# Slot records five chunks behind, more DMAs at the seams of the tail, and three tiles of types and masks in the message phase

## What is computed

```python
edge_index = jnp.stack([src, dst])
x = _layernorm(x + _L0_gnn_ref(x, edge_index, edge_attr_8, ...), axis=-1)     # attention, 8 heads
x = _layernorm(x + _L1_gnn_ref(x, edge_index, edge_type_16, ...), axis=-1)    # messages with an edge type of 16
x = _layernorm(x + _L2_gnn_ref(x, node_vec1, src, dst, edge_attr_4, edge_attr_8, ...), axis=-1)
x = _layernorm(x + _L3_gnn_ref(x, edge_index, L3_gnn_hyperedge_weight, ...), axis=-1)
```

```python
x = x @ W.T
e = segment_sum(Binv[edge_idx][:, None] * x[node_idx], edge_idx, num_segments=N_EDGES)
out = segment_sum(Dinv[node_idx][:, None] * e[edge_idx], node_idx, num_segments=N_NODES)
```

## Time and profile before

| | us |
|---|---|
| median of 3 runs (2760.82 to 2774.23) | 2763.07 |
| the profiled execution's own time | 2763.75 |
| its span, first to last instruction | 2762.0 |
| busy: PE / DVE / ACT / POOL | 1485.9 / 1676.3 / 879.7 / 1997.8 |

### The profile page before, as it was taken

One profiled execution on the slowest core, in us unless ns is written; L12 is line 12 of the kernel. 1 busy time (PEld: TensorE's weight loads), 2 busy tenths in 40 slices (PEclk: granted clock), 3 DMA queues, 4 the chain that ended last, 5 costly groups with the idle time before them and its releaser, 6 DMA issues. The chain is left out here.

```text
span 2762.0 us, 22483 instructions
## 1 busy us (share of the span) xinstructions
PE 1485.9 (54%) x4577; PEld 756.9 (27%) x4577; DVE 1676.3 (61%) x5026; ACT 879.7 (32%) x1963; POOL 1997.8 (72%) x1591
## 2 busy tenths in 40 slices
PE   6676548888736555554687736756663122221121
PEld 1233224444412222221333313422221121221110
DVE  8999837788916666684877754534444244334443
ACT  0111116666724455553466531211111111110000
POOL 5777677777358877764877727868887688878787
PEclk9989869999967677776889868978886555555555
DMA  1111133444244454444556547867887454443331
GB/s 25 16 27 28 21 93 110 124 126 114 69 110 120 101 119 121 114 90 102 100 133 145 129 104 211 263 193 224 230 226 182 104 124 122 116 109 83 85 85 45
DMA packets 357529, 320.56 MB, mean 116 GB/s; under 512 B 107129, under 2 KB 311824, under 8 KB 357377
## 3 DMA queue, kind: packets, MB, share of 16 engines
q1 hardware_dynamic: 256593, 247.94, 32.6%
q0 software_dynamic: 100800, 71.18, 13.8%
HBM read 222.19 MB, written 96.95 MB: 116 GB/s over the span
## 5 line engine op out<-in xcount | busy, mean ns | idle before, releaser
L2019 PE MATMUL tl_pX<-k_ident,tl_ga 125*128 125x125 f32 x400 | 92.4, 375 | 447.4 <-DMA tl_ga<-table_TE,k_s_idxE 256.3
L438 POOL DMA_INDIRECT tl_ga<-table_TE,k_s_idxE x200 | 245.5, 1228 | 80.3 <-issue 56.4
L2130 DVE TENSOR_TENSOR_SCAN tl_S<-tl_same,tl_S,tl_pX 128x500 f32<-128x500 f32 x96 | 120.2, 1252 | 244.8 <-issue 215.2
L2019 PEld LDWEIGHTS tl_pX<-k_ident,tl_ga 125*128 125x128 f32 x400 | 63.0, 192 | 465.4 <-DMA tl_ga<-table_TE,k_s_idxE 267.1
L438 POOL DMA_INDIRECT ms_ga<-table_T,k_idxS x100 | 140.5, 1405 | 65.1 <-issue 58.2
L1234 DVE TENSOR_TENSOR dr_o<-dr_x,tl_pMul 128x512 f32<-128x512 f32 x98 | 67.1, 685 | 185.8 <-DMA dr_x<-x 107.8
L1331 POOL DMA_INDIRECT k_pay<-table_ptab,k_clip x100 | 148.6, 1486 | 27.4 <-issue 27.1
L438 POOL DMA_INDIRECT at_ga<-x,at_srcI x100 | 130.3, 1303 | 43.2 <-issue 23.9
L438 POOL DMA_INDIRECT eq_ga<-table_T,k_idxS x100 | 125.6, 1256 | 48.7 <-issue 27.9
L438 POOL DMA_INDIRECT tl_ga<-table_TH,k_send x100 | 124.4, 1244 | 44.9 <-issue 44.2
L438 POOL DMA_INDIRECT at_gb<-x,at_dstI x100 | 126.5, 1265 | 38.8 <-issue 27.1
(11 more groups left out here) (430 smaller groups left out, 4726.4 us busy)
## 6 DMA issues: line engine op xcount, KB each, us to landing
dr_x<-x SPq DMA_DIRECT2D x97, 256.0 KB, 8.0
result<-dr_o SPq DMA_DIRECT2D x97, 256.0 KB, 5.4
dm_xT<-xT SPq DMA_DIRECT2D x32, 768.0 KB, 6.7
table_T<-at_y SPq DMA_DIRECT2D x50, 250.0 KB
table_T<-ms_y SPq DMA_DIRECT2D x50, 250.0 KB
table_T<-eq_y SPq DMA_DIRECT2D x50, 250.0 KB
tl_same<-table_dsame SPq DMA_DIRECT2D x50, 250.0 KB, 4.7
table_TE<-tl_y SPq DMA_DIRECT2D x50, 250.0 KB
```

Of the source, the lines that this page charges most:

```text
L438: nc.gpsimd.indirect_dma_start(out=buf[:, k, :], out_offset=None, in_=table, in_offset=bass.IndirectOffsetOnAxis(ap=index[:, CT * c + k:CT ...
L2019: last = nc.tensor.transpose(pX[j % 2][:, k * TP:(k + 1) * TP], ga[j % RG][:, k, :], K["ident"][0:TP, 0:TP])
L2130: nc.vector.tensor_tensor_scan(S[i][:], same[j % RM][:], pX[i][:, 0:CE], 0.0 if j % NC == 0 else S[1 - i][:, CE - 1:CE], ALU.mult, ALU.add ...
```

## The change

Three things. The message phase gets three copies of the types and of both masks instead of two, and SP issues them a turn earlier. The equivariant phase issues the slot records of a chunk five turns later (`LATE`), those of the last five chunks after the loop. In the tail four chunks of states instead of two stand at the first seam (`SEAM`), four chunks of scatters instead of two at the second, three instead of two at the third; the ring of o gets six copies, and the normalization of the target rows starts two turns earlier.

```diff
-        RG, RX, RU = 5, 4, 4
+        RG, RX, RU, RM = 5, 4, 4, 3
...
             def load_mask(c):
-                need(sp, s_S, c - 1)
-                need(sp, s_mean, c - 1)
-                sp.dma_start(same[c % 2][:], ...).then_inc(s_same[c % 2], 16)
-                sp.dma_start(deg[c % 2][:], ...).then_inc(s_same[c % 2], 16)
+                need(sp, s_S, c - RM + 1)
+                need(sp, s_mean, c - RM + 1)
+                sp.dma_start(same[c % RM][:], ...).then_inc(s_same[c % RM], 16)
+                sp.dma_start(deg[c % RM][:], ...).then_inc(s_same[c % RM], 16)
 
             def load_types(c):
-                need(sp, s_oneh, c - 1)
-                sp.dma_start(typ[c % 2][:], ...).then_inc(s_typ[c % 2], 16)
+                need(sp, s_oneh, c - RM + 1)
+                sp.dma_start(typ[c % RM][:], ...).then_inc(s_typ[c % RM], 16)
...
-            for s in range(-3, NC + 3):
-                if live(s + 3):
-                    load_types(s + 3)
-                if live(s + 1):
-                    load_mask(s + 1)
+            for s in range(-4, NC + 3):
+                if live(s + 4):
+                    load_types(s + 4)
+                if live(s + 2):
+                    load_mask(s + 2)
...
-        RG, RZ = 7, 4
+        RG, RZ, LATE = 7, 4, 5
...
-                if live(s):
-                    payload(s)
+                if live(s - LATE):
+                    payload(s - LATE)
+            for c in range(NC - LATE, NC):
+                payload(c)
             pool.wait_ge(s_pay, 16 * NT)
...
-        RG, RM, RL = 4, 3, 3
+        RG, RM, RL, RO = 4, 3, 3, 6
-        LN_EDGE = J_EDGE - 4
+        LN_EDGE = J_EDGE - 6
+        SEAM = 4
...
-            keep_states(0)
-            keep_states(1)
+            for c in range(SEAM):
+                keep_states(c)
             stored(pool, J_NODE)
             pool.wait_ge(s_zr, 16 * 2)
             for c in range(NC):
                 fetch(J_NODE + c)
-                if c + 2 < NC:
-                    keep_states(c + 2)
+                if c + SEAM < NC:
+                    keep_states(c + SEAM)
             for p in range(XR):
                 pool.wait_ge(dn.s_st[p], 16 * ((DQ - p + XR - 1) // XR + (p == (DQ - 1) % XR)))
-            scatter(0)
-            scatter(1)
+            for e in range(SEAM):
+                scatter(e)
             stored(pool, J_EDGE)
             for c in range(NC):
                 fetch(J_EDGE + c)
-                if c + 2 < NC - 2:
-                    scatter(c + 2)
-            scatter(NC - 2)
-            scatter(NC - 1)
+                if c + SEAM < NC - 3:
+                    scatter(c + SEAM)
+            for e in range(NC - 3, NC):
+                scatter(e)
             stored(pool, J_LAST)
```

More of the change, by code:

```diff
@@ L1252, in message_phase @@
         m, oF = (a.sb(n, [D, CE]) for n in ("m", "oF"))
-        xs, S, mean, same, deg = ([a.sb(f"{n}{i}", [D, CE]) for i in range(2)] for n in ("xs", "S", "mean", "same", "deg"))
-        typ, oneh = [a.sb(f"typ{i}", [16, CE], I32) for i in range(2)], [a.sb(f"oneh{i}", [128, CE]) for i in range(2)]
+        xs, S, mean = ([a.sb(f"{n}{i}", [D, CE]) for i in range(2)] for n in ("xs", "S", "mean"))
+        same, deg = ([a.sb(f"{n}{i}", [D, CE]) for i in range(RM)] for n in ("same", "deg"))
+        typ, oneh = [a.sb(f"typ{i}", [16, CE], I32) for i in range(RM)], [a.sb(f"oneh{i}", [128, CE]) for i in range(2)]
         n1, hg = (a.sb(n, [TP, 2 * CT, D]) for n in ("n1", "hg"))
@@ L1267, in message_phase @@
         s_ga, s_xt = [a.sem(f"ga{i}") for i in range(RG)], [a.sem(f"xt{i}") for i in range(RX)]
-        s_same, s_typ, s_st = ([a.sem(f"{n}{i}") for i in range(2)] for n in ("same", "type", "stored"))
+        s_same, s_typ = ([a.sem(f"{n}{i}") for i in range(RM)] for n in ("same", "type"))
+        s_st = [a.sem(f"stored{i}") for i in range(2)]
         block = ctx.enter_context(nc.Block())
@@ L1281, in load_mask @@
             def load_mask(c):
-                need(sp, s_S, c - 1)
-                need(sp, s_mean, c - 1)
-                sp.dma_start(same[c % 2][:], T["dsame"][:, CE * c:CE * c + CE].broadcast_to([D, CE])).then_inc(s_same[c % 2], 16)
-                sp.dma_start(deg[c % 2][:], T["rdeg"][:, CE * c:CE * c + CE].broadcast_to([D, CE])).then_inc(s_same[c % 2], 16)
+                need(sp, s_S, c - RM + 1)
+                need(sp, s_mean, c - RM + 1)
+                sp.dma_start(same[c % RM][:], T["dsame"][:, CE * c:CE * c + CE].broadcast_to([D, CE])).then_inc(s_same[c % RM], 16)
+                sp.dma_start(deg[c % RM][:], T["rdeg"][:, CE * c:CE * c + CE].broadcast_to([D, CE])).then_inc(s_same[c % RM], 16)
             def load_types(c):
-                need(sp, s_oneh, c - 1)
-                sp.dma_start(typ[c % 2][:], g["type_row"][:, CE * c:CE * c + CE].broadcast_to([16, CE])).then_inc(s_typ[c % 2], 16)
+                need(sp, s_oneh, c - RM + 1)
+                sp.dma_start(typ[c % RM][:], g["type_row"][:, CE * c:CE * c + CE].broadcast_to([16, CE])).then_inc(s_typ[c % RM], 16)
             def load_targets(c):
@@ L1463, in one_hot @@
             def one_hot(c):
-                dve.wait_ge(s_typ[c % 2], 16 * (c // 2 + 1))
+                dve.wait_ge(s_typ[c % RM], 16 * (c // RM + 1))
                 need(dve, s_psM, c - 1)
-                nc.vector.tensor_scalar(oneh[c % 2][0:16, :], typ[c % 2][:], kindf[:, 0:1], None, ALU.is_equal).then_inc(s_oneh, 1)
+                nc.vector.tensor_scalar(oneh[c % 2][0:16, :], typ[c % RM][:], kindf[:, 0:1], None, ALU.is_equal).then_inc(s_oneh, 1)
             def running(c):
@@ L1471, in running @@
                 dve.wait_ge(s_m, c + 1)
-                dve.wait_ge(s_same[i], 32 * (c // 2 + 1))
-                nc.vector.tensor_tensor_scan(S[i][:], same[i][:], m[:], 0.0 if c == 0 else S[1 - i][:, CE - 1:CE], ALU.mult, ALU.add).then_inc(s_S, 1)
+                dve.wait_ge(s_same[c % RM], 32 * (c // RM + 1))
+                nc.vector.tensor_tensor_scan(S[i][:], same[c % RM][:], m[:], 0.0 if c == 0 else S[1 - i][:, CE - 1:CE], ALU.mult, ALU.add).then_inc(s_S, 1)
             def averaged(c):
@@ L1478, in averaged @@
                 need(dve, s_psO, c - 1)
-                nc.vector.tensor_tensor(mean[i][:], S[i][:], deg[i][:], ALU.mult).then_inc(s_mean, 1)
+                nc.vector.tensor_tensor(mean[i][:], S[i][:], deg[c % RM][:], ALU.mult).then_inc(s_mean, 1)
             def residual(c):
@@ L1847, in tail_phase @@
         y = [a.sb(f"y{i}", [TP, CT, D]) for i in range(2)]
-        x, z, o = ([a.sb(f"{n}{i}", [TP, CT, D]) for i in range(RL)] for n in ("x", "z", "o"))
+        x, z = ([a.sb(f"{n}{i}", [TP, CT, D]) for i in range(RL)] for n in ("x", "z"))
+        o = [a.sb(f"o{i}", [TP, CT, D]) for i in range(RO)]
         st = a.sb("st", [TP, CT, 6])
@@ L1862, in tail_phase @@
         s_ga, s_same, s_fac, s_x, s_out, s_st = (
-            [a.sem(f"{n}{i}") for i in range(k)] for n, k in (("ga", RG), ("same", RM), ("fac", RM), ("x", RL), ("out", RL), ("stored", 2)))
+            [a.sem(f"{n}{i}") for i in range(k)] for n, k in (("ga", RG), ("same", RM), ("fac", RM), ("x", RL), ("out", RO), ("stored", 2)))
         s_gb, s_s4, s_rowT, s_row, s_rowst, s_rown, s_rowi, s_colT, s_idx, s_end, s_dinv, s_sl = (
@@ L1965, in scatter @@
             def scatter(e):
-                c, i = e % NC, e % RL
+                c, i = e % NC, e % RO
                 index = K["dst_end"] if e < NC else K["src_end"]
@@ L1973, in scattered @@
             def scattered(n):
-                for i in range(RL):
-                    pool.wait_ge(s_out[i], 64 * ((n - i + RL - 1) // RL))
+                for i in range(RO):
+                    pool.wait_ge(s_out[i], 64 * ((n - i + RO - 1) // RO))
             for c in range(NC):
@@ L2168, in finish @@
                 dve.wait_ge(s_mv, e + 1)
-                need(dve, s_out[e % RL], 64 * (e // RL))
-                normalize(nc, o[e % RL], z[e % RL], CT, mv[i], rs[i]).then_inc(s_o, 1)
+                need(dve, s_out[e % RO], 64 * (e // RO))
+                normalize(nc, o[e % RO], z[e % RL], CT, mv[i], rs[i]).then_inc(s_o, 1)
             def batch_norm():
```

## The result

The changed kernel took 2724.54 us (median of 4 runs, 2719.83 to 2730.55) beside 2765.7 for the kernel before on the same chip: a ratio of 0.9849, 95% interval 0.9814 to 0.9885, so 41 us less where 53 were forecast, and inside the range of the likeliest case (2692 to 2732). The profiled executions stand 44.0 us apart (spans 2762.0 and 2718.0).

A forecast was written before the change was run, and what follows sets the result against it. The prediction took a one-turn loop between types and y to bound the message phase, and POOL the edge stage. Terms -38 + 0 + 2 - 17 = -53 gave 2710 us; range 2692 to 2732, with neighbouring cases 2688 to 2742.

The forecast's parts named there:

- likeliest case: Whole kernel: message phase -24 to -53 and seam 3 -12 to -18, so 2692 to 2732 us; chance 0.50.
- Part 1: Message phase, three tiles of types and masks: types loop spans two turns, POOL becomes the bound by little; -38 us.
- best case: Message phase: POOL loses its 28.5 us of waits and DVE's lag behind the last gather shrinks; 53 us gained.
- worst case: Message phase: more POOL rows stretched by DVE operations, costing 29 us over 22 turns; 24 us of gain left.
- Part 2: Equivariant phase, slot records five chunks behind: cost 0, the scatters at the end covered by waiting; bounds -5 and +3.
- Part 3: Seam 1, target to node stage: eight more state gathers, 12.1 us, fill the 14.4 us wait; table lands as before.
- Part 4: Seam 2, node to edge stage: SP's issue, not the gather, is last, the wait stays; +2, bounds -12 and +4.
- the rival with seam 2 paying as well: Node stage's store depends on its last gather, so 12 us more gain and no +2: 2696 us; chance 0.17.
- Part 5: Seam 3, edge to last stage: eight fewer scatters in the edge stage, wait of 5.58 us gone; -17 us.
- a message phase that pays little: Second rival: loop moves to xT (y's end, xT load, squares) or SP stays late; 10 us won there, 2738; chance 0.18.
- no difference: Rival: message loop stays 18.6 us and the edge stage's store falls back; 2755 to 2770 us; chance 0.08.
- stretched rows of POOL: Slower rival: in the message phase a busier DVE stretches nearly all POOL rows to 2.10 us; 2818 us; chance 0.07.

The follow-up runs named there:

- four and eight chunks of payload moved: Changed kernel, payload gathers of the last four chunks moved into the equivariant phase: 0.9799; with three target-row loads at seam 1 too, four chunks 0.9767, eight 0.9742.
- Seam 2 as before: Changed kernel with normalization starting where it did before, two chunks of scatters at the second seam, four chunks of states kept at the first: 0.9880.
- the two runs with the states moved: State gathers of the last ten chunks put behind seam 2's scatters: on the changed kernel 2780.21 us, on it with three target-row loads at seam 1 1.0010.
- the first run with the states moved: Changed kernel with the 40 state gathers of the last ten chunks behind the scatters of seam 2: 2780.21 us in one run.

## Why the prediction came out as it did

**Part 1, right by 0.4 us, and partly by luck.** That the loop over the types breaks, that the masks' earlier issue adds nothing, that POOL takes over and that its rows don't stretch were all as written, and each has a row or a run of its own. The two pieces of the -38 were off in opposite directions. POOL gained 30.4 us up to its last gather, more than the best case's 28.5. Behind it the lag of DVE (last gather to last scan) was to shrink by 24, to 21 us, in the best case; it shrank by 8, to 37.4, since DVE has three full turns to do there and is busy nearly all the time. It is 37.4 us in all eleven kernels with this message phase, those with four and eight chunks of payload moved among them (1136.7 to 1174.1, 1132.5 to 1169.9). The middle of two bounds was right without either bound being: the worst case, stretched rows of POOL, didn't come at all.

**Part 2, right in kind.** No gain, as written, and the barrier was covered: 15.78 us of wait are left in front of it. The +5.4 of the profile is within the spread of that stage; the kernel with this edit alone is at 1.0012, which allows anything from nothing to 8 us of loss. Both lean to a loss of some 3 us, the upper bound of the part, and no run shows what would cause it.

**Part 3, right.** The wait was filled (14.36 to 2.43 us) and the table came no earlier.

**Part 4, the step that failed.** "The normalization starts two turns earlier, so two loads of x rows and its DVE work fall into turns that still have dense blocks: about 1 us each." Measured +7.8 for the term of +2. The count was right: one load stood ahead of dense loads before (at 2081.5), three do after. The price was wrong: two more of them cost some 4 us each, not 1, and DVE's work, which the sentence also names, nothing that shows. The row to size them by was there: the dense load that DVE waits 8.39 us for until 2093.10 is the one that stood behind that first load of target rows, in a turn of 14.4 us. The larger claim of the part held: SP's queue and the dense rows, not the gathers, decide when the last table of the stage is stored, and sixteen scatters in the seam left the wait as it was (14.68 to 15.81). Seam 2 as before bears it out, and so do the two runs with the states moved, so the rival with seam 2 paying as well is out. One wait wasn't foreseen in its size: the first scatter stood 10.08 us on POOL, under cover of that same seam. SP issues the last store of dense rows at 2079.73 and the scatter follows at 2084.33; the profile names no cause here, but in the first run with the states moved it puts the same wait down to the stores of dense rows (12.36 us).

**Part 5, right.** -16.9 for -17; the wait before the last stage is gone, and the chain kept up with the gathers.

The rivals with a message phase that pays little, with no difference and with stretched rows of POOL are out by the stage lengths. The message phase is not in the loop over xT at the margin that the second rival wanted, but it isn't far off: of 54 us taken off POOL 24 came through.

The experiments also give a kernel that beats both: three target-row loads at seam 1 and the payload of eight chunks in the equivariant phase, 2696.18 us, 0.9742 of the kernel before. It doesn't stand clear of the one with four chunks, whose interval overlaps.

## What to carry to other kernels

A wait that ends with a transfer issued behind the very result that it delays is a loop; one more buffer, with the issue a turn earlier, lets it span two turns, and the next bound can be sized in advance by adding up the busiest engine's rows and fixed gaps. Then count what every engine still has to do behind the last row of that one: here 37.4 us, whatever was taken off POOL. When a step is moved into turns that are short of transfers, price its loads by the wait of whoever is queued behind them, not by their bytes, and look for a seam where the queue and its readers stand still anyway: the same three loads cost 9 to 13 us in the dense turns, some 11 at the tail's start (the first dense block came that much later), and nothing that shows at seam 1.

## What the runs showed of the hardware

- A turn of 30 to 31 us, where 12 to 13 are usual, came in a stage of dense loads some 14 us after POOL had gone over to a single kind of small-row gather. The DMA engines show shares of 0.97 to 1.04 at 90 to 157 GB/s in it (the stage's usual is 241 at 0.88). Twice seen, at the same turn, in the two runs with the states moved; its cause stays open.
- POOL's indirect DMAs are slow beside some operations of DVE. Of the 200 in the message phase 51 take over 1.5 us before and 52 after, instead of 1.21. None of them is among the 79 and 66 that start with DVE idle, nor among the 40 and 39 that start under its statistics of rows, which read one tile. All 23 and 22 that start under its scan, which reads two, are slow.
- POOL's own operations hold up DVE. After, one multiplication of two tiles on DVE takes 4.06 us, where the other 24 of its line take 1.18 to 1.23, and the row spans both of POOL's tensor_tensors:

```profile
1182.86 4.06 DVE L1501 TENSOR_TENSOR ms_hg<-ms_n,ms_lg 125x1024 f32<-125x1024 f32 x1
...
1183.34 1.28 POOL L1341 TENSOR_TENSOR ms_xb<-ms_xt,ms_lb 125x512 f32<-125x512 f32 x1
1184.56 1.27 POOL L1342 TENSOR_TENSOR ms_xb<-ms_ga,ms_lb 125x512 f32<-125x512 f32 x1
```

The Trainium skill (SBUF — State Buffer, Who interferes with whom) says that a DVE instruction with two inputs in SBUF contends with a GpSimd one that reads SBUF, and this last row agrees with it in the direction that the prediction didn't think of: DVE is the one that waits.
